# A three-layer gated graph network on one core: where layer one counts, and where it gathers

## The chip, the cores and the metric

One core of a Trainium2 chip runs the whole program. The metric is the device time of one execution in microseconds.

## What is computed

`x` has 12500 rows of 128. It is layer-normalized, passed through a ReLU and a linear layer, and then three GRU layers run over a graph of 212500 edges, sorted by destination:

```python
for i in range(3):
    m = h @ weight[i]
    agg = segment_sum(m[src], dst, num_segments=n_nodes)
    h = gru_cell(agg, h, w_ih, w_hh, b_ih, b_hh)
return x + h
```

## The kernel before, in words

Edges are cut into 416 quads of 512 (four chunks of 128). Since edges are sorted by destination, a quad's destinations lie in a window of 36 nodes. 26 quads are a superblock, 16 superblocks in all. Messages are kept as three bf16 pieces, 768 bytes a row. Nodes are padded to 12544: 98 blocks of 128, 49 tiles of 256.

There are two ways to sum a quad's messages into its window.

*Gather.* POOL issues one indirect DMA for each chunk (L477, in a loop over steps of two quads, so eight a step) into a ring of four steps (`RING`); before a step it waits for PE's sums of four steps earlier (`s_sum`). DVE makes one-hots of the destinations (L1030, `make_onehot`, two steps ahead), PE multiplies 24 times (L716, `sum_chunk`), DVE adds two windows to `aggT` (L1053, `add_step`).

*Dense.* For a superblock's first 12 quads a matrix of counts (source node by window node) is multiplied with all messages, which lie in SBUF as `res` (7 piece loads of 1344 KB, L400): 98 blocks of three products of 432 columns (L751, `dense_block`), then 12 window adds (L1067, `add_superblock`). Counts come from memory in 14 slices of 768 KB a superblock (L414, `counts_in`), in four stage buffers.

Layer one gathers all 416 quads, in 208 steps. Layers two and three gather 14 quads of each superblock, in 112 steps, and take the other 12 from dense products, 98 x 16 blocks spread over the first 108 steps (`blocks_by`, `EARLY` = 4).

The counts do not depend on the layer. They are made once, during layer one, at steps 6 to 195 (`BUILD_FROM`, `BUILD_SPARE` = 12, `rounds_by`). For each of the 192 dense quads there are 7 rounds of 14 node blocks, 1344 rounds. DVE makes one-hots of the source node within its block (L1115, `block_onehot`, four a quad) and of block and window place (L1124, `quad_onehot`, four a quad of 1176 to 1862 elements), for whole quads, up to four quads ahead of PE (`XSLOTS`). PE multiplies four times a round (L733, `count_round`) into one of two psum banks, ACT evacuates (L597, `evacuate`) and SP stores 128 KB of counts (L424). An evacuation buffer holds a quad's seven rounds; there are two, and a quad waits for the stores of two quads earlier. These buffers and slots lie in `pieces_region`, over `res`, which layer one does not otherwise use.

The order of work is written out by hand, step by step, on every engine. PE in a step (`layer_steps`, L795): the sum of the step's gathered rows, the messages of the tile of two steps ago, the gates of a tile due in this step, then the counting rounds or dense blocks of the step. DVE (L1147): window adds, one-hots for two steps later, the phases of earlier tiles (L1101 to L1109, L1074, L1086), then the counting one-hots for the next step or a finished superblock's adds, then `gate_n` (L1095, L1097). ACT: tanh and clearing (L544, L546) of the last step's tile, copies of message pieces (L561, L567), gate activations, evacuations. `schedule` sets the step of each tile: after its last quad, and in layer one at least two steps apart (`TILE_SPACING`); a tile comes every 4.24 steps in layer one.

SP's queue holds in order: the pieces of layer one, each count store behind its evacuation, a wait for the last stores (L427), then the first four slices of layer two, its seven piece loads, each when its messages are stored (L436), and the other slices, each when its buffer is free. A layer's first gather waits until all messages of the layer before are stored.

Of the kernel before, what the change touches and what calls it, by code (L numbers as in the profile page):

```python
# [5 lines left out]
P = 128  # L6
# [21 lines left out]
XSLOTS_MOST = 4  # L28
EARLY = 4
BUILD_FROM = 6  # L30
BUILD_SPARE = 12
# [24 lines left out]
def gated_graph_layers(nc, x, src, dst, lin_wT, lin_b, weight, w_ihT, w_hhT, b_ih, b_hh, out, messages, states, counts):  # L56
# [13 lines left out]
    ALL_STEPS = NQ // 2  # L70
    GSB = GQ // 2
    G_STEPS = NSB * GSB
    STEP0 = [0, ALL_STEPS, ALL_STEPS + G_STEPS]
    STEPS = [ALL_STEPS, G_STEPS, G_STEPS]
# [3 lines left out]
    DENSE = NSB * NB  # L78
    PARTS = NB // (2 * HB)

    def quads_of(layer, s):
        if layer == 0:
            return 2 * s, 2 * s + 1
        first = SQ * (s // GSB) + DQ + 2 * (s % GSB)
        return first, first + 1

    def dense_quad(j):
        return SQ * (j // DQ) + j % DQ
# [5 lines left out]
    def blocks_by(s):  # L94
        return min(s * DENSE // (G_STEPS - EARLY), DENSE)

    def superblock_step(k):
        return next(s for s in range(G_STEPS) if blocks_by(s + 1) >= (k + 1) * NB)
# [4 lines left out]
    def ready_after(layer, t):  # L103
        quads = min(NQ, int(bound(t)) + 1)
        if layer == 0:
            return -(-quads // 2) - 1
        last = quads - 1
        k, offset = last // SQ, last % SQ
        steps = k * GSB - 1 if offset < DQ else k * GSB + (offset - DQ) // 2
        return max(steps, superblock_step(k))  # L110
# [19 lines left out]
    def dense_done(layer, s):  # L130
        if layer == 0:
            return 0
        k = sum(1 for k in range(NSB) if superblock_step(k) < s)
        return DQ * (NSB * (layer - 1) + k)

    with ExitStack() as ctx:
# [21 lines left out]
        iota_hi = sb("iota_round", [P, RW], F16)  # L158
# [24 lines left out]
        def half_at(reg, byte, n, dt):  # L183
# [7 lines left out]
        EVB = SLICES * SLW * 2  # L191
        ev = [half_at(region, b * EVB, SLICES * SLW, F16).rearrange("p (s w) -> p s w", w=SLW) for b in range(2)]
        XB = NB * sum(SUBW) * 2
        XIOTA = NB * max(SUBW)
        first_two = [(SUBLOW[c], SUBLOW[c] + SUBW[c]) for c in SUBORDER[:2]]
        assert first_two[0][0] == 0 and first_two[0][1] == first_two[1][0] and first_two[1][1] == W and XIOTA <= 2048
        XSLOTS = min(XSLOTS_MOST, (PB - 2 * EVB - 2 * XIOTA) // XB)
        xs = [[half_at(region, 2 * EVB + b * XB + NB * sum(SUBW[:c]) * 2, NB * SUBW[c], BF16) for c in range(QC)]
              for b in range(XSLOTS)]
        iota_x = half_at(region, 2 * EVB + XSLOTS * XB, XIOTA, F16)  # L200

# [36 lines left out]
        assert 2 * QC * P * 2 <= PL - DI and PL + 4 * DC <= SBYTES  # L238
# [80 lines left out]
        s_ast = [sem(f"counts_stored_{b}") for b in range(2)]  # L319
# [46 lines left out]
        def _(sp):  # L366
# [45 lines left out]
            def counts_in(v):  # L412
                k, j = (v % (NSB * SLICES)) // SLICES, v % SLICES
# [7 lines left out]
            for r in range(BUILD_ROUNDS):  # L421
                j, i = r // ROUNDS, r % ROUNDS
                sp.wait_ge(s_ev, r + 1)
                sp.dma_start(counts[j // DQ, 2 * i:2 * i + 2, :, j % DQ, :].rearrange("s p w -> p s w"),  # L424
                             ev[j % 2][:, 2 * i:2 * i + 2, :]).then_inc(s_ast[j % 2], 16)
            for b in range(2):
                sp.wait_ge(s_ast[b], 16 * ROUNDS * len(range(b, BUILDS, 2)))  # L427

            for layer in range(1, LAYERS):
                first = (layer - 1) * NSB * SLICES  # L430
# [58 lines left out]
        def _(act):  # L489
# [102 lines left out]
            def evacuate(r):  # L592
                j, i = r // ROUNDS, r % ROUNDS
                act.wait_ge(s_bld, r + 1)
                if i == 0 and j >= 2:
                    act.wait_ge(s_ast[j % 2], 16 * ROUNDS * (j // 2))
                nc.scalar.copy(ev[j % 2][:, 2 * i:2 * i + 2, 0:HB * W],  # L597
# [5 lines left out]
            act.wait_ge(s_pad, 2)  # L603
# [23 lines left out]
        def _(pe):  # L627
# [65 lines left out]
            def gate_products(layer, t, s):  # L693
# [6 lines left out]
                if layer:  # L700
                    pe.wait_ge(s_dadd, dense_done(layer, s))
# [20 lines left out]
            def count_round(r):  # L722
                j, i = r // ROUNDS, r % ROUNDS
                pe.wait_ge(s_x, j + 1)
# [5 lines left out]
                for k, c in enumerate(SUBORDER):  # L730
                    n = 2 * HB * SUBW[c]
                    x_round = xs[j % XSLOTS][c][:, n * i:n * (i + 1)].rearrange("p (b w) -> p b w", w=SUBW[c])
# [4 lines left out]
            def dense_block(layer, d):  # L737
                k, b = d // NB, d % NB
                kg = (layer - 1) * NSB + k
# [496 lines left out]
```

## Time and profile before

| | |
|---|---|
| median of three executions | 4676.5 us (4674.15 to 4683.16) |
| the profiled execution | 4676.84 us, its span 4675.0 us |
| PE busy | 3549.1 us, 76%, 27764 matmuls |
| POOL busy | 3441.7 us, 74% |
| DVE busy | 1806.5 us, 39% |
| ACT busy | 1102.3 us, 24% |
| DMA | 992.22 MB, mean 212 GB/s |
| granted clock of TensorE | 0.866 of full speed, mean |

The profile divides the span into 40 slices of 117 us. Each digit is a busy share in tenths:

```profile
PE   5256666666566666665289999999977999999998
...
ACT  4144444444344444443000110110110000000000
POOL 4777777777777777777577777777756777777775
PEclk8577888877787777777599999999988999999999
DMA  6566666666666666666578777887886877878886
```

The first slice is the prologue, the next 18 are layer one, then come layers two and three. POOL's digit 7 is one gather after another: each takes some 0.95 us, and 0.30 us pass before the next begins.

### The profile page before, as it was taken

What the parts mean: (1) busy time and instruction counts of PE and PEld (TensorE: products, weight loads), DVE (VectorE), ACT (ScalarE), POOL (GpSimd) and SP (SyncE); (2) the same over time, 40 slices, a digit from 0 to 9 for tenths busy, and PEclk for the clock granted to TensorE, in tenths of its full rate; (3) what the DMA queues carried; (4) which work ended last, traced back from release to release, by engine and by line L of the source; (5) the groups of instructions that cost most, each with busy time, mean ns of one, the idle gap of its engine ahead of it and who ended that gap; (6) DMA issues with size and microseconds to landing.
All of it is one profiled execution on the core that took longest, in us unless ns stands there. A gap on an engine that the chain in (4) does not pass through costs nothing.

```text
span 4675.0 us, 77190 instructions
## 1 busy us (share of the span) xinstructions
PE 3549.1 (76%) x27764; PEld 2254.5 (48%) x27765; DVE 1806.5 (39%) x7602; ACT 1102.3 (24%) x2162; POOL 3441.7 (74%) x3518
## 2 busy tenths in 40 slices
PE   5256666666566666665289999999977999999998
PEld 4134444444344444443145565565654555555555
DVE  7444454544454555443222232332331223222233
ACT  4144444444344444443000110110110000000000
POOL 4777777777777777777577777777756777777775
PEclk8577888877787777777599999999988999999999
DMA  6566666666666666666578777887886877878886
GB/s 214 170 165 175 176 181 179 177 178 168 167 173 176 181 178 180 173 176 198 138 230 258 254 251 256 257 257 250 263 261 200 260 249 257 265 239 263 258 254 185
DMA packets 744646, 992.22 MB, mean 212 GB/s; under 512 B 92856, under 2 KB 624952, under 8 KB 744248
## 3 DMA queue, kind: packets, MB, share of 16 engines
q1 hardware_dynamic: 489768, 582.80, 38.4%
q0 software_dynamic: 165888, 339.96, 27.8%
q10 hardware_dynamic: 88592, 64.25, 4.4%
q8 instruction: 237, 3.88, 0.3%
q14 instruction: 161, 1.32, 0.1%
HBM read 755.57 MB, written 231.08 MB: 211 GB/s over the span
## 4 chain that ended last, share of the span: by engine, by line
PE 42%; POOL 40%; issue 13%; DVE 3%; DMA 1%; DVEq 1%; ACT 0%; POOLq 0%; ACTq 0%; SPq 0%
POOL ring_region L477 40%; PE psum L751 32%; PE psum L704 3%; PE psum L716 2%; DVE aggT L1067 1%; DVEq L1020 1%; PE psum L676 1%; PE psum L678 1%; PE psum L677 1%; PE psum L689 1%; PE psum L649 1%; DMA ring_region<-messages,edge_src 1%; DVE pieces_region L855 0%; PE psum L659 0%; DMA temps<-states 0%
## 5 line engine op out<-in xcount | busy, mean ns | idle before, releaser
L477 POOL DMA_INDIRECT ring_region<-messages,edge_src x3456 | 3381.3, 978 | 1137.8 <-issue 1038.6
L751 PE MATMUL psum<-stage_region,pieces_region 128*128 128x432 f16 x9408 | 1766.1, 347 | 0.0
L751 PEld LDWEIGHTS psum<-stage_region,pieces_region 128*128 128x128 bf16 x9408 | 912.6, 97 | 793.2 <-issue 18.9
L1053 DVE TENSOR_TENSOR aggT<-aggT,psum 128x36 f32 x864 | 166.8, 193 | 2164.4 <-PE psum L716 1931.3
L733 PE MATMUL psum<-pieces_region,stage_region 128*128 128x238 bf16 (+2 forms) x5376 | 866.0, 311 | 148.9 <-ACT pieces_region L597 138.4
L716 PE MATMUL psum<-onehot,ring_region 128*128 128x36 bf16 x10368 | 345.5, 184 | 808.2 <-DMA ring_region<-messages,edge_src 791.7
L597 ACT CAST pieces_region<-psum 128x504 f16<-128x504 f32 x1344 | 746.7, 578 | 465.4 <-PE psum L733 450.9
L716 PEld LDWEIGHTS psum<-onehot,ring_region 128*128 128x128 bf16 x10368 | 326.3, 100 | 893.9 <-issue 843.9
L733 PEld LDWEIGHTS psum<-pieces_region,stage_region 128*128 128x128 bf16 x5376 | 526.0, 111 | 464.1 <-issue 328.2
L533 ACT ACTIVATE temps<-psum,small 128x256 f32<-128x256 f32 x147 | 69.6, 473 | 2132.4 <-PE psum L704 1966.7
L1030 DVE TENSOR_SCALAR onehot<-iota_block,edge_rel 128x36 bf16<-128x36 bf16 x3456 | 535.4, 255 | 2.3 <-issue 1.9
L1124 DVE TENSOR_SCALAR pieces_region<-pieces_region,stage_region 128x1666 bf16<-128x1666 f16 (+2 forms) x768 | 452.4, 652 | 0.0
L704 PE MATMUL psum<-aggT,wih 128*128 128x256 f32 x882 | 262.0, 442 | 55.8 <-DVE aggT L1067 55.8
L1115 DVE TENSOR_SCALAR stage_region<-iota_block,stage_region 128x128 bf16<-128x128 bf16 x768 | 148.2, 276 | 310.3 <-PE psum L733 310.2
L704 PEld LDWEIGHTS psum<-aggT,wih 128*128 128x128 f32 x882 | 203.1, 233 | 102.0 <-issue 64.3
L561 ACT CAST pieces_out<-psum 128x256 bf16<-128x256 f32 x98 | 36.5, 372 | 563.8 <-PE psum L689 530.9
L1067 DVE TENSOR_TENSOR aggT<-aggT,psum 128x36 f32 x384 | 74.1, 193 | 231.0 <-issue 123.3
L676 PE MATMUL psum<-temps,whh 128*128 128x256 f32 x294 | 124.8, 515 | 18.4 <-DMA temps<-states 18.4
L677 PE MATMUL psum<-temps,whh 128*128 128x256 f32 x294 | 112.7, 473 | 0.0
L678 PE MATMUL psum<-temps,whh 128*128 128x256 f32 x294 | 111.3, 468 | 0.0
L689 PE MATMUL psum<-wmsg,temps 128*128 128x128 f32 x392 | 90.0, 367 | 14.6 <-DVE temps L1109 9.8
L544 ACT ACTIVATE temps<-temps,small 128x256 f32<-128x256 f32 x147 | 74.7, 508 | 103.0 <-DVE temps L1097 102.6
(90 smaller groups left out, 1239.7 us busy)
## 6 DMA issues: line engine op xcount, KB each, us to landing
stage_region<-counts SPq DMA_DIRECT2D x448, 768.0 KB
counts<-pieces_region SPq DMA_DIRECT2D x1344, 128.0 KB
ring_region<-messages,edge_src POOLq DMA_INDIRECT x3456
pieces_region<-messages SPq DMA_DIRECT2D x21, 1344.0 KB, 17.5
temps<-states ACTq DMA_DIRECT2D x147, 128.0 KB
messages<-pieces_out ACTq DMA_DIRECT2D x98, 192.0 KB
states<-temps ACTq DMA_DIRECT2D x98, 128.0 KB
messages<-ring_region SPq DMA_DIRECT2D x25, 384.0 KB, 3.0
```

What stands on the lines that cost most here:

```text
L477: nc.gpsimd.indirect_dma_start(out=rows[:, n % RING, h * QC + c, :], out_offset=None, in_=messages[layer], in_offset=bass.IndirectOffsetOn ...
L597: nc.scalar.copy(ev[j % 2][:, 2 * i:2 * i + 2, 0:HB * W], psum[:, 6 + r % 2, 0:RW].rearrange("p (s w) -> p s w", w=HB * W)).then_inc(s_ev, 1)
L676: nc.tensor.matmul(GATE_R, whh[:, 0:P], state, start=True, stop=True)
L677: nc.tensor.matmul(GATE_Z, whh[:, P:2 * P], state, start=True, stop=True)
L678: nc.tensor.matmul(GATE_HN, whh[:, 2 * P:3 * P], state, start=True, stop=True).then_inc(s_hn, 1)
L704: nc.tensor.matmul(bank, wih[:, gate * P:(gate + 1) * P], nodes, start=alone, stop=True, skip_group_check=not alone).then_inc(s_gate, 1)
L716: mm = nc.tensor.matmul(window(n, h), rows[:, n % RING, i, k * P:(k + 1) * P], onehot[:, n % 3, i, :], start=(c == 0 and k == 0), stop=(c ...
L733: mm = nc.tensor.matmul(by_block[:, :, SUBLOW[c]:SUBLOW[c] + SUBW[c]], blocks_oh[j % 2][:, c, :], x_round, start=(k == 0), stop=True, skip ...
L751: mm = nc.tensor.matmul(psum[:, 6 + kg % 2, 0:DQ * W], res[:, b, piece * P:(piece + 1) * P], stage[v % ABUF][:, :, cols], start=(b == 0 an ...
L1030: made = nc.vector.tensor_scalar(onehot[:, n % 3, h * QC + c, :], iota_lo[:, 0:W], edge_rel[:, q * QC + c:q * QC + c + 1], None, ALU.is_equal)
L1053: nc.vector.tensor_tensor(cols, cols, window(n, h), ALU.add).then_inc(s_add, 1)
L1124: made = nc.vector.tensor_scalar(xs[j % XSLOTS][c], iota_x[:, 0:NB * SUBW[c]], keys[:, j * QC + c:j * QC + c + 1], -float(SUBLOW[c]), ALU. ...
```

## The change

Layer one takes the last six of its 16 superblocks (`FIRST_DENSE` = 3/8, `KD` = 6) as layers two and three do: ten superblocks are gathered whole, in 130 steps (`TURN`), and of the last six 14 quads each in 42 steps, with 588 dense blocks in the first 40 of them (`EARLY[0]` = 2). Layer one has 172 steps. All counts are still made, now at steps 6 to 127 (`BUILD_SPARE` = 2), the last six superblocks' first (`BUILD_ORDER`). At the turn PE waits for the last evacuation, SP for the last stores, and then SP loads the slices of the six superblocks.

`res` is in use in layer one now, so what counting needs moves to `stage_region`, and shrinks. A quad's one-hots are made in three groups of 3, 2 and 2 rounds (`GROUPS`, `group_onehot`, twelve instructions for four), with two group slots. A group waits for PE's rounds of two groups earlier; in a step DVE makes the groups up to one beyond that of the step's last round. The evacuation buffers hold one round, there are four (`EVSLOTS`), and an evacuation waits for the store of four rounds earlier. The iota for the one-hots is made in the prologue.

```diff
-XSLOTS_MOST = 4
-EARLY = 4
+GROUPS = ((0, 3), (3, 5), (5, 7))
+EVSLOTS = 4
+EARLY = (2, 4, 4)
+FIRST_DENSE = 3 / 8
 BUILD_FROM = 6
-BUILD_SPARE = 12
+BUILD_SPARE = 2
...
+    KD = int(NSB * FIRST_DENSE)
+    KG = NSB - KD
+    TURN = KG * SQ // 2
+    STEPS = [TURN + KD * GSB, G_STEPS, G_STEPS]
...
     def rounds_by(s):
-        last = ALL_STEPS - BUILD_SPARE
+        last = TURN - BUILD_SPARE
         return min(max(s - BUILD_FROM, 0) * BUILD_ROUNDS // (last - BUILD_FROM), BUILD_ROUNDS)
...
+    def groups_by(s):
+        done = rounds_by(s)
+        return 0 if done == 0 else min(group_of(done - 1) + 2, BUILDS * NG)
...
+    def blocks_by(layer, s):
+        count = len(DENSE_OF[layer]) * NB
+        steps = STEPS[layer] - DENSE_FROM[layer] - EARLY[layer]
+        return min(max(s - DENSE_FROM[layer], 0) * count // steps, count)
...
@@ block.sync
             for r in range(BUILD_ROUNDS):
                 j, i = r // ROUNDS, r % ROUNDS
                 sp.wait_ge(s_ev, r + 1)
-                sp.dma_start(counts[j // DQ, 2 * i:2 * i + 2, :, j % DQ, :].rearrange("s p w -> p s w"),
-                             ev[j % 2][:, 2 * i:2 * i + 2, :]).then_inc(s_ast[j % 2], 16)
-            for b in range(2):
-                sp.wait_ge(s_ast[b], 16 * ROUNDS * len(range(b, BUILDS, 2)))
+                sp.dma_start(counts[BUILD_ORDER[j // DQ], 2 * i:2 * i + 2, :, j % DQ, :].rearrange("s p w -> p s w"),
+                             ev[r % EVSLOTS]).then_inc(s_ast[r % EVSLOTS], 16)
+            for b in range(EVSLOTS):
+                sp.wait_ge(s_ast[b], 16 * len(range(b, BUILD_ROUNDS, EVSLOTS)))
+            for v in range(KD * SLICES):
+                slice_used(v - ABUF)
+                counts_in(v)
...
@@ block.scalar
             def evacuate(r):
-                j, i = r // ROUNDS, r % ROUNDS
                 act.wait_ge(s_bld, r + 1)
-                if i == 0 and j >= 2:
-                    act.wait_ge(s_ast[j % 2], 16 * ROUNDS * (j // 2))
+                if r >= EVSLOTS:
+                    act.wait_ge(s_ast[r % EVSLOTS], 16 * (r // EVSLOTS))
...
@@ block.tensor
             def count_round(r):
                 j, i = r // ROUNDS, r % ROUNDS
-                pe.wait_ge(s_x, j + 1)
+                g = group_of(r)
+                pe.wait_ge(s_x, g + 1)
...
+                if kg == 0 and b == 0:
+                    pe.wait_ge(s_ev, BUILD_ROUNDS)
...
                     if s < STEPS[layer] and layer == 0:
                         for r in range(rounds_by(s), rounds_by(s + 1)):
                             count_round(r)
-                    elif s < STEPS[layer]:
-                        for d in range(blocks_by(s), blocks_by(s + 1)):
+                    if s < STEPS[layer]:
+                        for d in range(blocks_by(layer, s), blocks_by(layer, s + 1)):
                             dense_block(layer, d)
...
@@ block.vector
-            def quad_onehot(j):
-                block_onehot(j)
-                if j >= XSLOTS:
-                    dve.wait_ge(s_bld, ROUNDS * (j + 1 - XSLOTS))
+            def group_onehot(g):
+                j, (low, high) = g // NG, ROUND_GROUPS[g % NG]
+                if g % NG == 0:
+                    block_onehot(j)
+                if g >= 2:
+                    dve.wait_ge(s_bld, rounds_of_groups(g - 2))
+                blocks = 2 * HB * (min(high, ROUNDS) - low)
                 for c in range(QC):
-                    made = nc.vector.tensor_scalar(xs[j % XSLOTS][c], iota_x[:, 0:NB * SUBW[c]],
-                                                   keys[:, j * QC + c:j * QC + c + 1], -float(SUBLOW[c]),
+                    col = quad_column(j) + c
+                    made = nc.vector.tensor_scalar(xs[g % 2][c][:, 0:blocks * SUBW[c]], iota_x[:, 0:blocks * SUBW[c]],
+                                                   keys[:, col:col + 1], -float(SUBLOW[c] + 2 * HB * low * SUBW[c]),
                                                    ALU.subtract, ALU.is_equal)
                 made.then_inc(s_x, 1)
...
                     if layer == 0 and s == BUILD_FROM - 1:
-                        for i in range(PARTS):
-                            dve.wait_ge(s_res[i], 16)
...
                     if layer == 0 and s < STEPS[0]:
-                        for j in range(quads_by(s + 1), quads_by(s + 2)):
-                            quad_onehot(j)
+                        for g in range(groups_by(s), groups_by(s + 1)):
+                            group_onehot(g)
```

## Rows read from the trace of the kernel before

**Rows 1.** The page: the chain that ended last, share of the span by engine.

```profile
PE 42%; POOL 40%; issue 13%; DVE 3%; DMA 1%; DVEq 1%; ACT 0%; POOLq 0%; ACTq 0%; SPq 0%
```

**Rows 2.** Windows: us; busy PE, PEld, DVE, ACT, POOL; PEclk; DMA share, GB/s.

```profile
220.00:1480.00 1260.00, 771.18 (x6703) 529.83 (x6700) 617.27 (x2367) 532.75 (x1013) 968.69 (x957) 0.79 0.64 174
...
2500.00:3440.00 940.00, 918.46 (x6794) 556.68 (x6792) 284.57 (x1359) 105.35 (x251) 706.55 (x740) 0.99 0.80 256
```

**Rows 3.** The chain of waits, 640 to 1480 us: share by line.

```profile
by line: POOL ring_region L477 76.4%; issue 22.9%; DMA ring_region<-messages,edge_src 0.6%; POOLq L474 0.2%; PE psum L716 0.1%
```

**Rows 4.** Groups of instructions by form, 640 to 1480 us.

```profile
L477 POOL DMA_INDIRECT ring_region<-messages,edge_src x639 | 646.2, 1011 | 194.7 <-issue 194.1 <-PE psum L716 0.6
...
L716 PE MATMUL psum<-onehot,ring_region 128*128 128x36 bf16 x1920 | 67.5, 190 | 268.5 <-DMA ring_region<-messages,edge_src 268.5
...
L1124 DVE TENSOR_SCALAR pieces_region<-pieces_region,stage_region 128x1862 bf16<-128x1862 f16 x80 | 56.9, 712 | 0.0
L1124 DVE TENSOR_SCALAR pieces_region<-pieces_region,stage_region 128x1176 bf16<-128x1176 f16 x80 | 42.5, 531 | 0.0
```

**Rows 5.** Timeline, step marks: start us, us, engine, line, operation, count [idle before].

```profile
206.96 0.61 PEld L716 LDWEIGHTS psum<-onehot,ring_region 128*128 128x128 bf16 x18 [12.11 <-issue]
...
1515.02 0.76 PEld L716 LDWEIGHTS psum<-onehot,ring_region 128*128 128x128 bf16 x24
...
2335.01 0.94 POOL L477 DMA_INDIRECT ring_region<-messages,edge_src  x1 [26.67 <-DMA messages<-pieces_out]
...
2346.50 0.58 PEld L716 LDWEIGHTS psum<-onehot,ring_region 128*128 128x128 bf16 x17 [20.71 <-issue]
...
2763.22 0.83 PEld L716 LDWEIGHTS psum<-onehot,ring_region 128*128 128x128 bf16 x24
...
3463.93 0.83 PEld L716 LDWEIGHTS psum<-onehot,ring_region 128*128 128x128 bf16 x24
```

**Rows 6.** Timeline of a tile step, 1142 to 1158 us.

```profile
1142.16 0.80 PEld L716 LDWEIGHTS psum<-onehot,ring_region 128*128 128x128 bf16 x24 [5.37 <-issue]
...
1143.64 1.20 DVE L1030 TENSOR_SCALAR onehot<-iota_block,edge_rel 128x36 bf16<-128x36 bf16 x8
...
1147.74 0.97 PEld L733 LDWEIGHTS psum<-pieces_region,stage_region 128*128 128x128 bf16 x8
...
1148.58 0.74 DVE L1115 TENSOR_SCALAR stage_region<-iota_block,stage_region 128x128 bf16<-128x128 bf16 x4 [3.75 <-PE psum L733]
...
1149.24 2.31 DVE L1124 TENSOR_SCALAR pieces_region<-pieces_region,stage_region 128x1176 bf16<-128x1176 f16 x4
...
1149.92 1.06 ACT L597 CAST pieces_region<-psum 128x504 f16<-128x504 f32 x2 [0.28 <-PE psum L733]
...
1151.26 1.06 ACT L597 CAST pieces_region<-psum 128x504 f16<-128x504 f32 x2 [0.28 <-PE psum L733]
```

**Rows 7.** The DMA queue's waits; the page's DMA issues, last column us to landing.

```profile
SPq L427 <- DMA counts<-pieces_region: 2.9, 1, 2.9
...
messages<-ring_region SPq DMA_DIRECT2D x25, 384.0 KB, 3.0
...
edge_src<-in_src SPq DMA_DIRECT2D x1, 832.0 KB, 8.6
```

**Rows 8.** Groups by form, 2500 to 3440 us; one step's products in the chain.

```profile
L477 POOL DMA_INDIRECT ring_region<-messages,edge_src x740 | 707.4, 956 | 233.7 <-issue 218.2 <-PE psum L716 15.4
...
2504.43 8.21 PE psum L751 x45
```

**Rows 9.** Timeline of the end of layer two, 3464 to 3521 us.

```profile
3464.72 56.15 SPq L400 DMA_DIRECT2D pieces_region<-messages  x7
...
3489.76 0.38 ACTq L558 DMA_DIRECT2D states<-temps  x1
...
3496.66 0.42 DVE L1109 TENSOR_TENSOR temps<-temps 128x256 f32<-128x256 f32 x1 [3.90 <-DMA states<-temps]
...
3521.29 0.94 POOL L477 DMA_INDIRECT ring_region<-messages,edge_src  x1 [50.46 <-DMA messages<-pieces_out]
```

More of the change, by code:

```diff
@@ L104, in ready_after @@
         quads = min(NQ, int(bound(t)) + 1)
-        if layer == 0:
-            return -(-quads // 2) - 1
         last = quads - 1
         k, offset = last // SQ, last % SQ
-        steps = k * GSB - 1 if offset < DQ else k * GSB + (offset - DQ) // 2
-        return max(steps, superblock_step(k))
+        i = k - DENSE_OF[layer][0]
+        if i < 0:
+            return last // 2
+        begun = DENSE_FROM[layer] + i * GSB
+        return max(begun - 1 if offset < DQ else begun + (offset - DQ) // 2, superblock_step(layer, i))
     def schedule(layer):
@@ L130, in dense_done @@
     def dense_done(layer, s):
[L131 to L134, printed above, removed]
+        done = sum(1 for i in range(len(DENSE_OF[layer])) if superblock_step(layer, i) < s)
+        return DQ * (DENSE0[layer] + done)
     with ExitStack() as ctx:
@@ L237, in gated_graph_layers @@
                              ).rearrange("p (c w) -> p c w", w=P) for b in range(2)]
-        assert 2 * QC * P * 2 <= PL - DI and PL + 4 * DC <= SBYTES
+        assert PL + 4 * DC <= SBYTES
+        XS0 = DI + 2 * QC * P * 2
+        XB = GBLOCKS * sum(SUBW) * 2
+        xs = [[half_at(stage_r, XS0 + b * XB + GBLOCKS * sum(SUBW[:c]) * 2, GBLOCKS * SUBW[c], BF16)
+               for c in range(QC)] for b in range(2)]
+        EV0 = XS0 + 2 * XB
+        ev = [half_at(stage_r, EV0 + b * 2 * SLW * 2, 2 * SLW, F16).rearrange("p (s w) -> p s w", w=SLW)
+              for b in range(EVSLOTS)]
+        assert EV0 + EVSLOTS * 2 * SLW * 2 <= SBYTES
         outside = real_dst
@@ L318, in gated_graph_layers @@
         s_ev = sem("counts_left_psum")
-        s_ast = [sem(f"counts_stored_{b}") for b in range(2)]
+        s_ast = [sem(f"counts_stored_{b}") for b in range(EVSLOTS)]
         s_al = [sem(f"counts_loaded_{b}") for b in range(ABUF)]
@@ L412, in counts_in @@
             def counts_in(v):
[L413 removed]
+                used, j = v // SLICES, v % SLICES
+                k = DENSE_OF[0][used] if used < KD else (used - KD) % NSB
                 sp.dma_start(stage[v % ABUF], counts[k, j]).then_inc(s_al[v % ABUF], 16)
@@ L699, in gate_products @@
                 pe.wait_ge(s_add, added(layer, s))
-                if layer:
+                if dense_done(layer, s):
                     pe.wait_ge(s_dadd, dense_done(layer, s))
@@ L738, in dense_block @@
                 k, b = d // NB, d % NB
-                kg = (layer - 1) * NSB + k
+                kg = DENSE0[layer] + k
                 v = kg * SLICES + b // HB
@@ L1036, in add_step @@
             def add_step(layer, s, n):
-                if s % 2 == 0 and layer == 0:
-                    for k, value in enumerate(lows_of(2 * s, 4)):
-                        lows[2 * s + k] = value
-                if layer and s % GSB % 2 == 0:
-                    first = quads_of(layer, s)[0]
+                first = quads_of(layer, s)[0]
+                if layer == 0 and s < TURN:
+                    if s % 2 == 0:
+                        for k, value in enumerate(lows_of(first, min(4, 2 * (TURN - s)))):
+                            lows[first + k] = value
+                elif (s - DENSE_FROM[layer]) % GSB % 2 == 0:
                     for k, value in enumerate(lows_of(first, min(4, SQ - first % SQ))):
@@ L1166, in layer_steps @@
                     if layer == 0 and s < STEPS[0]:
-                        for j in range(quads_by(s + 1), quads_by(s + 2)):
-                            quad_onehot(j)
-                    if layer:
-                        for k in range(NSB):
-                            if superblock_step(k) == s:
-                                add_superblock(layer, k, s)
+                        for g in range(groups_by(s), groups_by(s + 1)):
+                            group_onehot(g)
+                    for i in range(len(DENSE_OF[layer])):
+                        if superblock_step(layer, i) == s:
+                            add_superblock(layer, i, s)
                     if s in tiles_at:
```

83 lines of the change are left out of this document (42 added, 41 removed).

## The prediction

> **What bounds the kernel now.** I read the page's chain first: it is 42% PE and 40% POOL [rows 1], so two stages with different limits lie behind the averages. The windows by stage part them: in layer one POOL is busy 969 of 1260 us while PE is busy 771 us at a mean granted clock of 0.79 of full speed (a mixture of 1.2 and 2.4 GHz); in layer two PE is busy 918 of 940 us at 0.99, 2.4 GHz nearly throughout [rows 2]. The chain restricted to 640-1480 us says it outright: 76.4% POOL L477 plus 22.9% issue, which is POOL's own gap between gathers [rows 3]. So layer one runs at POOL's pace: 639 gathers in 840 us, 80 steps of eight, 10.5 us a step. PE waits for rows 268.5 us there, 3.4 us a step, so its own work is 7.1 us a step, with 7.07 counting rounds in it [rows 4]. The step marks are the first L716 weight load of a step: step 6 at 206.96, step 130 at 1515.02 (10.55 us a step), next layer's gathers from 2335.01 us [rows 5]. In layers two and three POOL needs 10.1 us and PE as much, with 14.5 dense blocks a step; they are not touched.
>
> **What is removed.** Layer one has 172 steps for 208: 288 gathers, 36 steps. At 10.5 us that is 378 us of POOL. Counting keeps its 1344 rounds, but they now lie in steps 6 to 127, 11.02 a step for 7.07 (before: steps 6 to 195). The sum therefore depends on what a counting step will cost.
>
> **A counting step, engine by engine.**
> PE and ACT: neighbouring pairs of evacuations start at 1149.92 and 1151.26, 0.67 us a round, each pair ending in a PE wait for ACT [rows 6]. Another 3.95 rounds add 2.6 us: PE's work goes from 7.1 to 9.8 us, which POOL's 10.5 would still cover.
> DVE: a quad's four slot instructions take 2.31 us [rows 6]; from the 1176- and 1862-wide forms an element costs (712-531)/686 = 0.264 ns [rows 4], so 6370 elements are 1.68 us and the rest, 0.16 us, is each instruction's own. Twelve instructions for four keep the elements: 3.6 us a quad. With 0.74 us of block one-hots [rows 6] and 1.57 quads a step that is 6.8 us for 3.1 now. DVE is busy 617 of 1260 us, 5.1 us a step [rows 2], so it comes to 8.8: covered, but only two group slots (2 or 3 rounds each) let it run ahead, where four quads did.
> The count stores: this is the term that I expect to decide. An evacuation now waits for the store of four rounds earlier to land; before, for one of at least eight rounds earlier. The store's time has one direct row: the wait at the end of counting, 2.9 us for the last one; a store of three times the size, 384 KB, took 3.0 us [rows 7]. So four slots turn in 0.58 (evacuation) + 0.03 (issue, an estimate) + 2.9 + 0.1 (wake, an estimate) = 3.6 us, 0.91 us a round. Bounds: 0.67, if the landings are hidden by the pauses, and 1.3, if a store takes 4.5 us because counting writes 56% more a step. I take 0.91: the row is of a store of just this kind, issued behind others.
> The Trainium skill (DMA: Bandwidth & Descriptors, Anatomy of one DMA) puts the fixed cost of a DMA at about 2.0 us, most of it the write receipt. By that the slots would turn in 2.7 us, 0.68 a round, no slower than now, and the sum would be that of the first rival; the row says 2.9, and the row is used.
> A step without a tile is then 11.02 x 0.91 = 10.05 us; the 0.9 us of step sums hides in it, since two psum banks hold rounds that ACT has yet to take. A tile step has 5.6 us before its first round (1142.16 to 1147.74) [rows 6], of which two rounds, 1.8 us, are hidden; slots that came free in the pause give 0.8 back: +3.0 us. ACT's tanh, clearing and pieces copies and DVE's late first group in the two steps behind add some 1.9 us a tile (an estimate from operations of 0.4 to 0.6 us like those of [rows 6]; bounds 0 and 4). A tile comes every 4.24 steps: 4.9 / 4.24 = 1.15. **A counting step: 11.2 us**, over POOL's 10.5, so the ring fills and PE's loop sets the pace.
>
> **The turn.** Steps 128 and 129 count nothing. Their rows lie ready in the full ring, so PE has three step sums and one tile's gates before the first dense block: some 7.4 us (0.9 a sum, 5.6 with gates [rows 6]). SP takes longer: the last evacuation and store, 3.5 us, then four slices of 768 KB. No row has a slice's landing: bounds are 3.0 us (384 KB) and 8.6 us (832 KB) [rows 7]; nearer in size is 832, I take 8. **11.5 us** from the last round to the first dense block (7.4 to 12.5).
>
> **The dense part.** 588 blocks in 40 steps, 14.7 a step. Layer two does 14.5 a step, and its first 40 steps took 2763.22-2346.50 = 416.7 us, 10.42 each [rows 5]; 0.18 blocks more, at 8.21/45 us a product [rows 8], add 0.1: 421 us. Slice loads ride beside as in layer two, at a DMA share of 0.80 [rows 2].
>
> **The end of layer one.** Four tiles stand behind the last dense block, as in layer two, where it took 3463.93 to 3521.29, 57.4 us, with seven piece loads (1344 KB each) issued at its start, among which a state store took 6.9 us [rows 5, 9]. Layer one's own end was cheap, POOL idle 26.7 us [rows 5]; it inherits the dear one because piece loads can no longer start while gathering goes on. Its tiles stand two steps apart for one; these steps are empty, so I add nothing (bounds -10, +20).
>
> Dropped at nothing: the wait for pieces, the four iota steps and wide memsets at step 5 (one late step in 208); the extra iota of the prologue beside a 2.7 us POOL reduction; dense-product waits, already met.
>
> **Sum.** 207.0 + 122 x 11.2 = 1573.4; + 11.5 = 1584.9; + 421 = 2005.9, the end of the dense blocks; + 57.4 = 2063.3 for 2335.0 now: 271.7 us less, say 272. Layers two and three keep their 2340 us. The profiled execution took 4676.8 us (its span 4675.0), the median of three is 4676.5, so the same base: **4405 us**. Each 0.1 us of a counting step is 12.2 us.
>
> **Rivals.**
> *Slots never bind.* Pauses let the stores land, PE stays under POOL: 10.55 us a step, so step 130 begins at 1515.0 as now, the slices loaded in time: 1515.0 + 421 + 57.4 = 1993.4, 341.6 us less, 4335. For it: PE's 9.8 us, and that POOL absorbs uneven steps by its ring of four. Against: 2.9 us for four rounds.
> *DVE and PE in lockstep.* DVE starts its groups some 2.7 us after a step's sum starts (sum 1142.16, one-hots done 1144.84 [rows 6]), has 6.8 us to do and one group in hand; a tile's three blend operations come first in the next step. If each step loses 0.8 us more to that, 122 x 0.8 = 98 us more, 4503. For: 8.8 busy us in 11.2; against: at 0.91 a round PE wants a group each 2.1 us and DVE makes one in 1.45.
> *The gathers slow.* L477 averages 1011 ns in the counting and 956 without [rows 4, 8], some 0.44 us a step for 3.1 us of counting one-hots. In proportion 6.8 us would make POOL's step 11.0, still under 11.2.
> The Trainium skill (SBUF — State Buffer, Who interferes with whom) has VectorE and GpSimd lock each other out of a shared port for whole instructions. Taken fully, each one-hot microsecond would be one more of POOL: 10.0 + 6.8 = 16.8 us a step, 122 x 5.6 = 683 us more, 5088 us. The trace shows a seventh of it.
> *Slower than before: the store loop.* Place: the wait of L597 for the store four rounds back. The saving is gone when a counting step reaches 11.2 + 272/122 = 13.4 us. The tiles' 1.15 us left aside, 12.3 us is 1.11 a round, a store of 3.7 us. At 4.5 us, 1.3 a round, a step is 15.5 us and the time 4930. For: a 128 KB state store among slice loads was waited for until 3496.66, issued at 3489.76, 6.9 us [rows 9]; against: no slices are loaded while counting goes on.
>
> **How the numbers follow.** Forecast 0.50 (4365 to 4450 by its own bounds); slots never bind 0.22; lockstep 0.17; the port taken fully 0.02; slower by the store loop 0.06; other small mishaps of either sign 0.03. The range takes in the first three, 4330 to 4530. A measurement of this kernel tells about 0.2% (9 us) from no change: faster 0.91, within 0.01, slower 0.08.
>
> **What would show it.** Right: in the counting window POOL's idle before L477 is released by PE L716, and L597's idle by the counts' stores; step 6 to 128 takes 1366 us; dense steps 10.5; POOL idle near 50 us at the end of layer one. Slots not binding: PE L716 still waits for DMA rows. Lockstep: PE L733 waits for the DVE slot line. Wrong altogether if the counting steps exceed 13.4 us or the dense steps 12.

## The result and the profile after

The changed kernel takes 4409.4 us (median; 4395.6 to 4417.2) and the kernel before 4678.3 us beside it: a ratio of 0.943, 95% interval 0.9417 to 0.9447, 269 us less. The forecast was 4405 us. The profiled execution took 4412.1 us, its span is 4410.1.

From the page of the changed kernel: the span, the busy times, the granted clock in 40 slices, and the shares of the chain by engine and by line (the new lines are L504 for L477, L742 for L716, L761 for L733, L781 for L751, L623 for L597, L1166 for L1124).

```profile
span 4410.1 us, 81110 instructions
...
PE 3705.5 (84%) x28664; PEld 2305.8 (52%) x28665; DVE 1996.3 (45%) x8849; ACT 1107.3 (25%) x2162; POOL 3148.9 (71%) x3230
...
PEclk8688898888889989997999999999979999999999
...
PE 62%; DMA 12%; DVE 10%; POOL 6%; issue 5%; ACT 4%; DVEq 2%; ACTq 0%; POOLq 0%; SPq 0%
PE psum L781 40%; DMA counts<-stage_region 10%; PE psum L761 7%; POOL ring_region L504 6%; PE psum L730 5%; PE psum L742 4%; ACT stage_region L623 4%; DVE stage_region L1166 3%; DVE onehot L1063 2%; PE psum L702 1%; DVE aggT L1101 1%; PE psum L703 1%; PE psum L704 1%; DVEq L1053 1%; DVE stage_region L1153 1%
```

In the chain POOL has fallen from 40% [rows 1] to 6%, and something has come in that was not there: the counts' stores, 10% of the whole span. Windows of the changed kernel, the counting steps and the dense part of layer one:

```profile
core 0: us, PE busy (x) PEld busy (x) DVE busy (x) ACT busy (x) POOL busy (x), PEclk, DMA share, GB/s
203.60:1607.40 1403.80, 1002.39 (x8768) 669.05 (x8769) 1066.63 (x4494) 815.13 (x1516) 1016.33 (x998) 0.88 0.76 206
1611.00:2021.00 410.00, 397.67 (x2965) 237.51 (x2964) 116.37 (x577) 37.82 (x94) 303.96 (x319) 0.99 0.81 261
```

While it counts PE is busy 71% of the time (61% before [rows 2]) and its mean granted clock is 0.88 for 0.79. The chain of waits inside the counting steps, shares by line, and below it who waited for whom in 640 to 1480 us (us in total, times, longest):

```profile
by line: DMA counts<-stage_region 30.8%; PE psum L761 20.8%; ACT stage_region L623 11.4%; DVE stage_region L1166 9.7%; DVE onehot L1063 4.8%; issue 4.3%; PE psum L742 3.8%; DVE stage_region L1153 2.8%; PE psum L730 2.7%; DVE aggT L1087 1.7%
```

```profile
PEld psum L761 <- DVE stage_region L1166: 193.6, 214, 3.8
...
ACT stage_region L623 <- DMA counts<-stage_region: 156.1, 222, 2.9
...
PE psum L761 <- ACT stage_region L623: 138.2, 252, 2.9
...
PE psum L761 <- DVE stage_region L1166: 93.8, 71, 3.6
POOL ring_region L504 <- PE psum L742: 68.7, 38, 4.5
```

Before, 640 to 1480 us of this stage read 76.4% POOL and 22.9% issue [rows 3]. Now 31% of it is the flight of a count store, and POOL waits for PE (68.7 us of 840), which is to say that the ring is full. Two kinds of wait lie side by side: ACT for stores (156 us of 840), and PE for one-hots (94 us; 194 at its weight loads). The step marks in the timeline of the changed kernel:

```profile
203.62 0.37 PEld L742 LDWEIGHTS psum<-onehot,ring_region 128*128 128x128 bf16 x10 [9.18 <-issue]
...
1607.39 1.36 PEld L742 LDWEIGHTS psum<-onehot,ring_region 128*128 128x128 bf16 x48
...
1611.17 0.87 PEld L742 LDWEIGHTS psum<-onehot,ring_region 128*128 128x128 bf16 x24
...
1612.40 19.60 SPq L438 DMA_DIRECT2D stage_region<-counts  x7
...
1616.80 9.88 PE L781 MATMUL psum<-stage_region,pieces_region 128*128 128x432 f16 x42 [4.66 <-DMA stage_region<-counts]
...
2021.30 0.83 PEld L742 LDWEIGHTS psum<-onehot,ring_region 128*128 128x128 bf16 x24
...
2074.57 0.94 POOL L504 DMA_INDIRECT ring_region<-messages,edge_src  x1 [62.71 <-DMA messages<-pieces_out]
```

The line at 1607.39 holds the rows of steps 128 and 129 together (x48), and step 130 begins at 1611.17: the ring was full, and PE took the two steps in 3.8 us.

| stage | forecast us | measured us |
|---|---|---|
| start of step 6 | 207.0 | 203.6 |
| 122 counting steps | 1366.4 (11.2 each) | 1403.8 (11.51 each) |
| to the first dense block | 11.5 | 9.4 |
| 40 dense steps | 421 | 404.5 |
| end of layer one | 57.4 | 53.3 |
| layers two and three | 2340.0 | 2335.5 |
| span | 4403.3 | 4410.1 |

### The profile page after: what moved, and what is told of

The parts are those of the page before. It is cut to its first block, busy times and chain, and to the rows that moved or that the text cites. A ratio compares the mean times of both kernels' runs of the same rounds, so it can differ in the third digit from the quotient of the medians.

```text
span 4410.1 us, 81110 instructions
## 1 busy us (share of the span) xinstructions
PE 3705.5 (84%) x28664; PEld 2305.8 (52%) x28665; DVE 1996.3 (45%) x8849; ACT 1107.3 (25%) x2162; POOL 3148.9 (71%) x3230
## 4 chain that ended last, share of the span: by engine, by line
PE 62%; DMA 12%; DVE 10%; POOL 6%; issue 5%; ACT 4%; DVEq 2%; ACTq 0%; POOLq 0%; SPq 0%
PE psum L781 40%; DMA counts<-stage_region 10%; PE psum L761 7%; POOL ring_region L504 6%; PE psum L730 5%; PE psum L742 4%; ACT stage_region L623 4%; DVE stage_region L1166 3%; DVE onehot L1063 2%; PE psum L702 1%; DVE aggT L1101 1%; PE psum L703 1%; PE psum L704 1%; DVEq L1053 1%; DVE stage_region L1153 1%
## 5 line engine op out<-in xcount | busy, mean ns | idle before, releaser
L504 POOL DMA_INDIRECT ring_region<-messages,edge_src x3168 | 3088.4, 975 | 1166.2 <-issue 944.5
L781 PE MATMUL psum<-stage_region,pieces_region 128*128 128x432 f16 x11172 | 2096.8, 347 | 4.7 <-DMA stage_region<-counts 4.7
L781 PEld LDWEIGHTS psum<-stage_region,pieces_region 128*128 128x128 bf16 x11172 | 1083.0, 97 | 945.4 <-issue 21.6
L761 PE MATMUL psum<-stage_region 128*128 128x238 bf16 (+2 forms) x5376 | 846.6, 302 | 401.4 <-ACT stage_region L623 232.4
L623 ACT CAST stage_region<-psum 128x504 f16<-128x504 f32 x1344 | 752.6, 579 | 521.1 <-DMA counts<-stage_region 273.2
L761 PEld LDWEIGHTS psum<-stage_region 128*128 128x128 bf16 x5376 | 504.0, 108 | 724.1 <-DVE stage_region L1166 328.2
L1166 DVE TENSOR_SCALAR stage_region<-iota_group,stage_region 128x476 bf16<-128x476 f16 (+5 forms) x2304 | 700.3, 369 | 208.8 <-PE psum L761 203.8
L1063 DVE TENSOR_SCALAR onehot<-iota_block,edge_rel 128x36 bf16<-128x36 bf16 x3168 | 486.8, 253 | 2.7 <-issue 2.3
L742 PE MATMUL psum<-onehot,ring_region 128*128 128x36 bf16 x9504 | 304.2, 179 | 110.2 <-DMA ring_region<-messages,edge_src 93.6
L742 PEld LDWEIGHTS psum<-onehot,ring_region 128*128 128x128 bf16 x9504 | 298.9, 97 | 164.6 <-issue 106.8
L702 PE MATMUL psum<-temps,whh 128*128 128x256 f32 x294 | 101.5, 428 | 21.7 <-DMA temps<-states 21.7
L1129 DVE SCALAR_TENSOR_TENSOR temps<-psum,small,temps 128x256 f32<-128x256 f32 x147 | 70.4, 479 | 51.1 <-ACT temps L560 37.9
L703 PE MATMUL psum<-temps,whh 128*128 128x256 f32 x294 | 92.9, 399 | 0.0
L704 PE MATMUL psum<-temps,whh 128*128 128x256 f32 x294 | 92.2, 397 | 0.0
```

Of the source, the lines that this page charges most:

```text
L504: nc.gpsimd.indirect_dma_start(out=rows[:, n % RING, h * QC + c, :], out_offset=None, in_=messages[layer], in_offset=bass.IndirectOffsetOn ...
L623: nc.scalar.copy(ev[r % EVSLOTS][:, :, 0:HB * W], psum[:, 6 + r % 2, 0:RW].rearrange("p (s w) -> p s w", w=HB * W)).then_inc(s_ev, 1)
L702: nc.tensor.matmul(GATE_R, whh[:, 0:P], state, start=True, stop=True)
L703: nc.tensor.matmul(GATE_Z, whh[:, P:2 * P], state, start=True, stop=True)
L742: mm = nc.tensor.matmul(window(n, h), rows[:, n % RING, i, k * P:(k + 1) * P], onehot[:, n % 3, i, :], start=(c == 0 and k == 0), stop=(c ...
L761: mm = nc.tensor.matmul(by_block[:, :, SUBLOW[c]:SUBLOW[c] + SUBW[c]], blocks_oh[j % 2][:, c, :], x_round, start=(k == 0), stop=True, skip ...
```

## The experiments

They ask what makes a counting step 11.5 us: the loop of four stores (forecast), DVE and PE in lockstep over two group slots (rival), or the gathers, slowed by one-hots (rival). The table has what all of them gave, each as one execution but for the last; step times are from the starts of step 6 and step 128 in the timelines (122 steps between them).

| kernel | us | kernel before beside it | us a counting step | mean ns of a gather, 640 to 1480 us |
|---|---|---|---|---|
| the change | 4412.1 (profiled) | 4678.3 | 11.51 | 1020 |
| eight store buffers | 4364.1 | 4681.7 | 10.91 | 1057 |
| four group slots | 4375.2 | 4681.7 | 11.12 | 1051 |
| both | 4371.4 | 4681.7 | 10.96 | 1061 |
| a quarter of the one-hots | 4392.1 | 4681.7 | 11.34 | 954 |
| both, a quarter of the one-hots | 4270.3 | 4676.2 | 10.15 | 959 |
| three store buffers | 4580.0 | 4676.2 | 12.92 | 1031 |
| small buffers, nothing dense | 4731.7 | 4676.2 | 10.68 | 1028 |
| two groups a quad, eight stores | 4409.1 (4 runs) | 4676.2 | 11.26 | 1101 |

### Eight stores, three stores, four groups, both: first runs

```diff
-EVSLOTS = 4
+EVSLOTS = 8
...
```

This is the edit for eight stores; three stores has `EVSLOTS = 3` and nothing else, and the edit for four groups stands below. Four new buffers lie in the last of the seven piece blocks, which is loaded a second time behind the first four slices.

> Eight store buffers for four (the four new ones lie in the last piece block of pieces_region, which is loaded again after counting); all else as in the changed kernel (4412.1 us, 11.51 us a counting step). Store loop theory: four slots of 3.6 us set the step; with eight the wait of ACT for the counts' stores goes to near nothing and a step falls to what PE and DVE need, 10.6 to 10.9 us: 4300 to 4340 us. Lockstep theory (DVE and PE bound through two one-hot slots): the wait of ACT turns into a wait for PE, the step stays at 11.2 to 11.5 us: 4375 to 4412 us.

> Three store buffers for four, nothing else. Store loop theory: 3.6 us over three slots is 1.2 us a round, 13.2 us for 11 rounds and about 14 us a step with the tiles: 4412 + 122 x 2.5 = 4720 us (4680 to 4760). Lockstep theory: stores have slack at four, so three cost only part of it, a step of 11.6 to 12.3 us: 4425 to 4510 us.

> Four one-hot group slots for two (the two new ones lie in the last two piece blocks, loaded again after counting), four store buffers as in the change. Store loop theory: a step stays at 11.2 us or more, 4375 to 4412 us. Lockstep theory: PE's wait for the one-hots (94 us of 840 in the changed kernel) goes, and a step falls to 10.6 to 10.9 us: 4300 to 4340 us.

> Eight store buffers and four group slots together. Both theories: nothing but POOL and PE's own work is left, POOL's ring is no longer full, a counting step is 10.6 to 10.7 us, 4300 to 4315 us. If this is no faster than the better of the two alone, one of the two limits was the only one; if each alone gives little and both give 100 us, the limits lie in series.

They took 5486.6, 5543.3, 5482.6 and 5484.7 us, but the kernel before took 5771.1 us beside them, 23% more than anywhere else. In the first of them the instructions of POOL, ACT and DVE took no longer than in its second run (a gather 976 ns for 985 over the whole span, an evacuation 579 in both), but every engine idled more, in dense layers too, and 15% of the chain went to a releaser that the profile does not tell. So none of the expected times can be held against them; why they were slow is not known. The four were run again.

### Eight store buffers

> Eight store buffers for four, again, since the kernel before took 5771 us beside the first run and 4678 us elsewhere. Store loop theory: the wait of ACT for the counts' stores goes, a counting step falls to 10.6 to 10.9 us: 4300 to 4340 us beside 4678 for the kernel before. Lockstep theory: 11.2 to 11.5 us a step, 4375 to 4412 us.

It took 4364.1 us, 48 less, and 10.91 us a step. The chain within 640 to 1480 us and the gathers:

```profile
by line: POOL ring_region L522 59.6%; issue 18.1%; PE psum L779 6.3%; DVE stage_region L1184 5.2%; DMA ring_region<-messages,edge_src 1.9%; DVE onehot L1081 1.6%; DVE stage_region L1171 1.5%; PE psum L760 1.2%; ACT stage_region L641 0.8%; A
```

```profile
L522 POOL DMA_INDIRECT ring_region<-messages,edge_src x618 | 653.0, 1057 | 188.3 <-issue 187.1 <-PE psum L760 1.2
```

The stores have left the chain. The step lies just above what the store loop theory gave it (10.6 to 10.9), the time 24 us above the end of its range. For the most part it is not PE or DVE that ends the step: POOL and its gaps are 78% of the chain, and a gather takes 1057 ns.

The counting steps took 71 us less in all, the time only 48, because steps 128 to 169 took 435 us for 414. The change reaches step 128 with its ring full, 3.9 steps of rows that PE has yet to sum, and passes steps 128 and 129 in 3.8 us. At POOL's pace the ring holds 1.5 steps there, and the same two steps take 21.1 us. The dense steps take 413.5 us for 404.5; this kernel loads a piece block a second time there, so that difference need not be the ring's. A counting step that is brought down to the pace of its gathers gives part of the gain back.

### Four group slots

```diff
+GSLOTS = 4
-        return 0 if done == 0 else min(group_of(done - 1) + 2, BUILDS * NG)
+        return 0 if done == 0 else min(group_of(done - 1) + GSLOTS, BUILDS * NG)
...
-                if g >= 2:
-                    dve.wait_ge(s_bld, rounds_of_groups(g - 2))
+                if g >= GSLOTS:
+                    dve.wait_ge(s_bld, rounds_of_groups(g - GSLOTS))
...
```

The two new slots lie in the last two piece blocks, which are loaded a second time.

> Four one-hot group slots for two, four store buffers, again for the same reason. Store loop theory: 4375 to 4412 us. Lockstep theory: PE's wait for the one-hots goes, 10.6 to 10.9 us a step, 4300 to 4340 us.

4375.2 us, 37 less, 11.12 us a step: both theories get a part. Its chain and its waits in 640 to 1480 us:

```profile
by line: DMA counts<-stage_region 51.2%; ACT stage_region L642 15.2%; PE psum L780 13.3%; issue 4.4%; PE psum L761 2.3%; PE psum L749 2.3%; DVE pieces_region L1185 2.2%; DVE stage_region L1185 1.6%; PE psum L721 1.0%; DVE stage_region L1172
```

```profile
ACT stage_region L642 <- DMA counts<-stage_region: 216.4, 326, 2.8
PE psum L780 <- ACT stage_region L642: 213.6, 378, 2.8
...
PEld psum L780 <- DVE stage_region L1185: 71.8, 78, 3.0
...
PEld psum L780 <- DVE pieces_region L1185: 55.6, 82, 2.4
```

PE's waits for one-hots are 127 us at the weight loads for 194, and 19 us at the products for 94. ACT now waits 216 us for stores, for 156: what the one-hots no longer held up, the stores did. With most of the one-hot waits out of the way the loop of four stores gives 11.1 us, and this is what 11.2 stood for, though its parts were others (below).

### Both

> Eight store buffers and four group slots, again for the same reason. Both theories: POOL's own pace or PE's own work is left, 10.6 to 10.7 us a step, 4300 to 4315 us; if no faster than the better of the two alone, one limit was the only one.

4371.4 us, within 0.2% of eight stores alone and 56 us above the end of its range. The chain and the gathers:

```profile
by line: POOL ring_region L523 74.2%; issue 21.3%; DMA ring_region<-messages,edge_src 1.8%; PE psum L780 0.5%; PE psum L761 0.4%; DVE pieces_region L1185 0.3%; PE psum L749 0.2%; ACT pieces_region L642 0.2%; DVE stage_region L1185 0.2%; POO
```

```profile
L523 POOL DMA_INDIRECT ring_region<-messages,edge_src x616 | 653.8, 1061 | 187.8 <-issue 186.9 <-PE psum L761 0.9
```

POOL and issue are 95.5% of the chain: 8 x (1.061 + 0.30) = 10.9 us. The floor of 10.5 us was wrong, because the gathers themselves have become slower. As with eight stores, the turn takes back some of the gain (steps 128 and 129: 22.4 us).

### A quarter of the one-hots

```diff
-                for c in range(QC):
+                for c in range(QC) if g < 2 * NG else range(1):
                     col = quad_column(j) + c
                     made = nc.vector.tensor_scalar(xs[g % 2][c]...
```

This kernel leaves out three of a group's four slot one-hots.

> The changed kernel with three of the four slot one-hots of a group left out after the sixth group (PE counts with what lies in the slot, so the counts of those chunks are not the reference's); stores, evacuations and matmuls are all there. DVE has some 4 us a step less to do. Store loop theory: the loop of four stores is untouched, a step stays at 11.0 to 11.4 us, 4350 to 4400 us. Lockstep theory: 10.6 us, 4300 to 4320 us. Port theory: L504's mean falls from 1020 ns to 970 or less.

4392.1 us, 11.34 a step: the store loop's range, not the lockstep's. The chain and the gathers:

```profile
by line: DMA counts<-stage_region 47.6%; PE psum L761 16.3%; ACT stage_region L623 14.6%; issue 4.1%; PE psum L742 3.4%; DVE onehot L1063 2.6%; PE psum L730 2.5%; PE psum L702 1.1%; DVE stage_region L1153 1.0%; DVE aggT L1087 0.9%; PE psum 
```

```profile
L504 POOL DMA_INDIRECT ring_region<-messages,edge_src x594 | 566.5, 954 | 274.2 <-issue 179.0 <-PE psum L742 95.2
```

The loop of stores and evacuations has taken over the chain (62% with L623), and a gather costs 954 ns for 1020, with all stores in flight: it is the one-hots that slow it. The faster gathers gained nothing, since POOL was not the bound. The 20 us go with shorter waits for one-hots, but not all of these went (152 us at the weight loads for 194, 46 at the products for 94): there are still two group slots, and DVE waits 334 us for PE. Four slots with all one-hots did more, 11.12.

### Both, and a quarter of the one-hots

> Eight store buffers and four group slots (4371 us, POOL-bound at 10.96 us a counting step, gathers of 1061 ns), and three of a group's four slot one-hots left out after the twelfth group, so that the counts of those chunks are not the reference's. If the one-hots slow the gathers: L523's mean falls to about 955 ns, POOL's step is (0.955 + 0.30) x 8 = 10.05 us, and the time is 4371 - 0.9 x 122 = 4260 us (4250 to 4290). If DMA traffic slows them: L523 stays at 1050 ns, 4355 to 4375 us.

4270.3 us, 10.15 us a step, as worked out from the one-hots (4250 to 4290):

```profile
by line: POOL ring_region L523 69.3%; issue 22.3%; DMA ring_region<-messages,edge_src 3.7%; PE psum L800 1.6%; PE psum L780 0.7%; PE psum L761 0.7%; ACT stage_region L642 0.3%; PE psum L749 0.3%; ACT pieces_region L642 0.3%; POOLq L520 0.2%
```

```profile
L523 POOL DMA_INDIRECT ring_region<-messages,edge_src x666 | 638.4, 959 | 203.0 <-issue 201.1 <-PE psum L761 1.8
```

Against the kernel with both and all one-hots that is 101 us and 102 ns a gather less; 102 ns x 8 x 122 = 100 us. More was moved in the same time (DMA share 0.84 for 0.79 in 640 to 1480 us), so DMA traffic is not what slows them.

### Three store buffers

> Three store buffers for four in the changed kernel, again, since its first run was beside a kernel before of 5771 us. Store loop: 3.6 us over three slots is 1.2 us a round, a step of 13.3 to 14.2 us, 4630 to 4740 us. If the store loop were only a part that overlaps with the one-hot waits: 11.8 to 12.5 us, 4450 to 4530 us.

The edit is `EVSLOTS = 3`. 4580.0 us, 12.92 us a step, between the two ranges, so neither theory has the size right. The chain:

```profile
by line: DMA counts<-stage_region 41.4%; PE psum L761 16.5%; ACT stage_region L623 13.7%; DVE stage_region L1166 5.9%; issue 4.2%; PE psum L742 3.4%; DVE onehot L1063 3.2%; PE psum L730 2.3%; DVE stage_region L1153 1.9%; PE psum L702 1.2%; 
```

Stores and L623 are 55% of it. 12.92 us for 11.02 rounds is 1.17 us a round at most, so three slots turn in 3.5 us or less. The trace has it directly: where L623 waited for a store in 640 to 1480 us, the evacuation three rounds earlier had begun 3.3 us before (median of 357). That is 12.0 us for 11.02 rounds, and 0.9 us a step for all the rest; with four buffers the same sum leaves 1.5.

### Small buffers, nothing dense

```diff
-FIRST_DENSE = 3 / 8
+FIRST_DENSE = 0
...
```

(One more line lets `ready_after` do without dense superblocks.)

> The change's small buffers and groups alone: no superblock of layer one is dense, 208 steps, counting at steps 6 to 205, 6.7 rounds a step. Store loop and lockstep theories: at 6.7 rounds neither is full, POOL sets the pace as before. Twelve slot one-hots for four make 4.2 us of them a step for 3.1, which by the gathers' slowing (0.44 us a step for 3.1 us) is 0.15 us a step: 4682 + 30 = 4712 us (4690 to 4730). If small buffers cost something of their own: over 4750 us.

4731.7 us, 55 more than the kernel before where 30 were expected. Gathers and PE's wait for rows:

```profile
L504 POOL DMA_INDIRECT ring_region<-messages,edge_src x631 | 648.8, 1028 | 192.3 <-issue 192.0 <-PE psum L742 0.3
...
L742 PE MATMUL psum<-onehot,ring_region 128*128 128x36 bf16 x1896 | 66.9, 190 | 196.4 <-DMA ring_region<-messages,edge_src 196.4
```

PE waits for rows 196 us (268.5 before [rows 4]) and POOL sets the pace, at 1028 ns a gather for 1011: 0.14 us a step, as expected. Step 170 begins 33 us later than before. Nearly all of the rest, 24 us, comes from there to the next layer's first gather. Counting now ends ten steps later and pushes stores, slices and pieces towards the layer's end; that this is the cause was not tested.

### A candidate: eight stores, two groups a quad

```diff
-GROUPS = ((0, 3), (3, 5), (5, 7))
-EVSLOTS = 4
+GROUPS = ((0, 4), (4, 7))
+EVSLOTS = 8
+GSLOTS = 3
```

> A candidate: eight store buffers, all in the last two piece blocks, three group slots, and groups of 4 and 3 rounds, so eight slot one-hots a quad for twelve (statistics scratch moved to make room for the longer iota). DVE has 1.0 us a step less to do. If one-hots slow the gathers: L523 1061 to 1045 ns, 10.8 us a step, 4350 us (4335 to 4365). If not: 4364 to 4375 us as with both.

4409.1 us (ratio 0.9425, interval 0.9403 to 0.9448), the same as the change and outside both ranges: a miss. DVE did less (576 us busy in 640 to 1480 us for 666 with both), but a gather costs more:

```profile
L524 POOL DMA_INDIRECT ring_region<-messages,edge_src x598 | 658.3, 1101 | 182.2 <-issue 181.6 <-PE psum L762 0.6
```

At 11.26 us a step its counting steps still took 30 us less than the change's; steps 128 to 169, at POOL's pace, took 25 us more (438.7 for 413.9) and used it up.

The timeline of this kernel shows a slow gather. Rows are start us, us, engine, line, operation, count, idle before:

```profile
1101.56 0.94 POOL L524 DMA_INDIRECT ring_region<-messages,edge_src  x1 [0.30 <-issue]
...
1103.37 0.75 DVE L1175 TENSOR_SCALAR stage_region<-iota_block,stage_region 128x128 bf16<-128x128 bf16 x4
...
1104.02 1.56 DVE L1188 TENSOR_SCALAR pieces_region<-iota_group,stage_region 128x672 bf16<-128x672 f16 x4
1104.06 3.58 POOL L524 DMA_INDIRECT ring_region<-messages,edge_src  x1 [0.30 <-issue]
...
1105.49 1.33 DVE L1188 TENSOR_SCALAR stage_region<-iota_group,stage_region 128x504 bf16<-128x504 f16 x4
...
1106.72 0.93 DVE L1175 TENSOR_SCALAR stage_region<-iota_block,stage_region 128x128 bf16<-128x128 bf16 x4
...
1107.36 1.61 DVE L1188 TENSOR_SCALAR stage_region<-iota_group,stage_region 128x672 bf16<-128x672 f16 x4
```

A gather that began at 1104.06 took 3.58 us, while DVE's instructions went back to back. The kernel before has the same, one gather over a whole quad's slot one-hots:

```profile
1090.24 0.74 DVE L1115 TENSOR_SCALAR stage_region<-iota_block,stage_region 128x128 bf16<-128x128 bf16 x4
...
1090.87 3.10 POOL L477 DMA_INDIRECT ring_region<-messages,edge_src  x1 [0.30 <-issue]
1090.89 2.27 DVE L1124 TENSOR_SCALAR pieces_region<-pieces_region,stage_region 128x1176 bf16<-128x1176 f16 x4
```

## Why the prediction was right

**The time and its range.** 4405 against 4409. The errors of the stages nearly cancel: +37 us in counting, -17 in the dense steps, -14 in the rest. That they do is luck: the sum is better than its parts.

**The counting step.** 11.2 against 11.51. That the four stores' loop would bound it holds: three slots cost 1.4 us a step more, eight 0.6 less, and the chain names the store. The price of the loop holds too. In the change's trace L623 waited for a store before 239 of 804 rounds in 640 to 1480 us; the evacuation four rounds earlier had then begun 3.6 us before, with 2.95 us between the store's issue and its landing (medians); 3.6 and 2.9 were forecast. Waits pick out the slower stores, so these are high if anything.

What was mis-sized stands beside the loop, twice and with opposite signs. The 35 counting steps with no tile in them or in the two steps before took 11.03 us on average, where 11.02 x 0.91 = 10.05 had been worked out. With four group slots they took 10.51, so half of that miss is waits for one-hots, which the forecast gave to a rival alone; what the other half is was not tested. Tiles then add 11.51 - 11.03 = 0.48 us a step where 1.15 were given. One reason is PE's part: a tile step's first round came 3.6 us after the step's start (mean), 5.2 before, and 5.6 in the step that the forecast read. Those rows come from a stage at a mean clock of 0.79, a good part of it at 1.2 GHz; rows of before and, below, of after:

```profile
L704 PE MATMUL psum<-aggT,wih 128*128 128x256 f32 x114 | 38.7, 492 | 0.0
...
L676 PE MATMUL psum<-temps,whh 128*128 128x256 f32 x38 | 22.9, 705 | 0.0
```

```profile
L504 POOL DMA_INDIRECT ring_region<-messages,edge_src x586 | 597.8, 1020 | 243.2 <-issue 174.5 <-PE psum L742 68.7
...
L730 PE MATMUL psum<-aggT,wih 128*128 128x256 f32 x108 | 27.0, 387 | 0.0
...
L702 PE MATMUL psum<-temps,whh 128*128 128x256 f32 x36 | 12.4, 425 | 0.0
```

With the engine busier (granted clock 0.88 for 0.79) a gate product takes 387 ns for 492, a state product 425 for 705.

**Lockstep.** Over all counting steps, four group slots alone bring 11.51 to 11.12 us. The rival was thus a part of the likeliest case, 0.39 us of it, and not another one.

**Slots never bind (4335).** No kernel with all its one-hots came near: with both limits away 4371, and step 130 began at 1564.2 us where this rival had 1515.0. The pace it was given, POOL's 10.55, no longer held: the gathers were slower.

**The gathers slow.** The forecast made POOL's step 11.0 us and called it covered. It measured 10.9 where it was the bound; the proportion was good. By the Trainium skill (SBUF — State Buffer, Who interferes with whom) VectorE, in its modes that take both port pairs, and GpSimd shut each other out for whole instructions. The trace fits that for single gathers (3.58 us for one that otherwise takes 0.95), but not for each of them: the full price, 16.8 us a step, was not there.

**The Trainium skill's 2.0 us** (DMA: Bandwidth & Descriptors, Anatomy of one DMA) would have had the slots turn in 2.7 us and not bind. The section takes its figure from DMAs that GpSimd issues, and adds bytes / 436e3 us, 0.3 for 128 KB; by that estimate they turn in 3.0 us. The trace agrees with neither: where ACT waited, a store landed 2.95 us after its issue with four buffers and 2.6 with three. The row's 2.9 us was the better price.

**The turn.** 9.4 us for 11.5, two errors that partly cancel. The last evacuation and store took 5.0 us (1607.39 to the first slice's issue at 1612.40) for 3.5. A slice was taken at 8 us; from its issue to the first product at 1616.80 are 4.4 us.

**The dense steps.** 10.1 us for 10.5, which was layer two's 10.42 and 0.1. The changed kernel's own trace says why. Layer two starts with its ring empty: in its first 40 steps PE is busy 399 of 418 us, and POOL's gathers and the gaps behind them are a third of the chain (25.6% and 8.8%). Layer one's dense steps start with the ring that counting has filled: PE is busy 397 of 404.5 us, and no gather stands among the lines of the chain, of which dense products are 79%. The forecast took layer two's pace over and with it layer two's waits for rows.

**The end.** 53.3 for 57.4, taken over from layer two [rows 9]. POOL is idle 62.7 us there, for 26.7 before [rows 5] and some 50 forecast.

**Stays open.** Whether eight stores alone beat the change by more than chance from run to run: 4364.1 is one execution, 1% under the change's median and outside its four (4395.6 to 4417.2), and each was compared with another execution of the kernel before (ratios 0.932 and 0.943). How much of 11.51 is stores and how much one-hots can't be split: each removed alone is worth 0.6 and 0.4 us, both together 0.55, because POOL's 10.9 lies under both.

## What to carry to other kernels

When work is packed into fewer steps its buffers turn faster: work out the time of one turn (use, issue, landing, wake), divide by the slots, and put that beside the engines' busy times before choosing how many. A bound of the kernel before is no floor for the kernel after when the engine beside it takes on more of what slows it. Where three limits lie within 5%, removing one shows the next, so remove them two at a time before believing what either is worth. And count what lies in a ring when a stage ends: the next stage starts on that stock, and a faster stage that leaves it empty gives some of its gain back.

## What the runs showed of the hardware

A gather (one indirect DMA issued by POOL) takes 0.95 us, the median in every kernel. Beside VectorE's bf16 one-hots most still do, and a few take far longer, up to 3.6 us while a dozen VectorE instructions go back to back. So it is not the one-hots' sum alone that counts. Eight longer instructions a quad cost 1101 ns a gather (65 of 598 over 1.2 us, the longest 3.58) where twelve shorter ones, with 16% more VectorE busy time, cost 1061 (93 of 616, the longest 2.56). The changed kernel, where DVE waits often for PE's rounds, has 1020 (44 of 586). That a gap between one-hots is what lets POOL in would fit this, but was not tested by itself.

A store of 128 KB from SP's queue, among others like it, landed some 3 us after its issue where the kernel waited for it (median 2.95, a tenth of them over 4.2).
